# Attention and feed-forward layer: a zeroing matmul pair ahead of each y accumulation, and output stores moved six steps later in the down projection

## The reference, cut to what matters

```python
# attention without softmax: causal linear attention, 16 heads of 64
qkv = x @ Wqkv_w.T + Wqkv_b
scores = jnp.einsum('bhld,bhmd->bhlm', q, k * scale)
y = jnp.einsum('bhlm,bhmd->bhld', scores * causal, v)
a = y @ out_w.T + out_b
x = _layernorm(x + a)
# feed-forward, hidden 3072, int weights scaled by 1/127
h = jax.nn.silu(x @ wg.T) * (x @ wu.T)
x = _layernorm(x + h @ wd.T)
```

## Time and profile before

| what | us |
|---|---|
| median of 2 runs | 2166.96 (2164.74 to 2169.18) |
| the profiled execution, its own time | 2171.79 |
| span of its slowest core, the one shown (core 3) | 2170.2 |
| spans of the eight cores | 2148.2 to 2170.2 |
| mean granted TensorE clock, core 3 | 0.913 of full speed |

### The profile page before, as it was taken

One profiled execution on the slowest core, in us unless ns is written; L12 is line 12 of the kernel. 1 busy time (PEld: TensorE's weight loads), 2 busy tenths in 40 slices (PEclk: granted clock), 3 DMA queues, 4 the chain that ended last, 5 costly groups with the idle time before them and its releaser, 6 DMA issues.

```text
span 2170.2 us, 26434 instructions; the slowest of 8 cores (2148.2 to 2170.2 us)
## 1 busy us (share of the span) xinstructions
PE 1785.8 (82%) x9492; PEld 833.3 (38%) x9492; DVE 406.8 (19%) x803; ACT 400.3 (18%) x679; POOL 284.8 (13%) x263
## 2 busy tenths in 40 slices
PE   0775868998888788999868787999878778899985
PEld 0342433443334343444324343444333434344431
DVE  0212121121121222121121212212112122211111
ACT  0131221111013222111012223211101312211101
POOL 2032242100003121000002212000000302100001
PEclk9986989999888889999989897999989878899998
DMA  9119089974520102223541100322462010132264
GB/s 171 23 12 125 1 97 140 172 136 127 179 83 1 39 1 78 78 78 95 168 126 39 39 1 20 103 75 76 122 187 79 10 35 1 30 83 78 84 174 150
DMA packets 127935, 180.00 MB, mean 83 GB/s; under 512 B 58800, under 2 KB 58816, under 8 KB 127424
## 3 DMA queue, kind: packets, MB, share of 16 engines
q1 hardware_dynamic: 73728, 151.03, 24.0%
q0 software_dynamic: 54080, 27.28, 11.7%
HBM read 188.76 MB, written 35.65 MB: 103 GB/s over the span
## 4 chain that ended last, share of the span: by engine, by line
PE 69%; DMA 12%; DVE 6%; issue 5%; ACT 4%; POOL 3%; DVEq 0%; SPq 0%; ACTq 0%; POOLq 0%
PE pF L731 14%; PE pF L739 14%; PE pF L411 11%; PE pF L819 11%; PE pF L593 7%; PE pF L470 5%; DMA wdr<-wd_scr 5%; DMA wo_bf<-woT 2%; PE pF L386 2%; DMA wu_scr<-wuT 2%; ACT v_tm L478 2%; DVE h1f L639 1%; PE pF L513 1%; DMA wgr<-wg_scr 1%; ACT sqs L690 1%
## 5 line engine op out<-in xcount | busy, mean ns | idle before, releaser
L819 PE MATMUL pF<-wdr,h_fm 128*128 128x512 bf16 x1472 | 352.9, 397 | 59.4 <-DMA wdr<-wd_scr 58.7
L731 PE MATMUL pF<-x_fm,wgr 128*128 128x512 bf16 x1536 | 362.8, 379 | 10.2 <-DMA wgr<-wg_scr 6.4
L739 PE MATMUL pF<-x_fm,wur 128*128 128x512 bf16 x1536 | 362.8, 379 | 1.9 <-DMA wur<-wu_scr 1.9
L411 PE MATMUL pF<-x_fm,wqkv_bf 128*128 128x512 bf16 x1024 | 241.6, 401 | 13.2 <-DVE x_fm L396 8.1
L819 PEld LDWEIGHTS pF<-wdr,h_fm 128*128 128x128 bf16 x1472 | 143.9, 101 | 266.4 <-issue 121.1
L753 DVE TENSOR_TENSOR h_fm<-silu_s,pF 128x512 bf16<-128x512 bf16 x192 | 131.9, 687 | 531.9 <-PE pF L739 531.9
L731 PEld LDWEIGHTS pF<-x_fm,wgr 128*128 128x128 bf16 x1536 | 149.5, 98 | 191.3 <-issue 13.1
L739 PEld LDWEIGHTS pF<-x_fm,wur 128*128 128x128 bf16 x1536 | 150.0, 98 | 183.9 <-issue 3.9
L750 ACT ACTIVATE silu_s<-pF 128x512 bf16<-128x512 f32 x192 | 114.6, 597 | 549.9 <-PE pF L731 549.8
L593 PE MATMUL pF<-wo_bf,y_fm 128*128 128x512 bf16 x512 | 174.4, 516 | 0.0
L709 POOL TENSOR_SCALAR out_sb<-h1f,stats 128x1024 f32<-128x1024 f32 x32 | 38.2, 1193 | 993.3 <-DVE stats L707 980.9
(11 more groups left out here) (76 smaller groups left out, 943.4 us busy)
## 6 DMA issues: line engine op xcount, KB each, us to landing
wdr<-wd_scr SPq DMA_DIRECT2D x256, 256.0 KB, 3.2
wgr<-wg_scr SPq DMA_DIRECT2D x96, 256.0 KB, 2.7
wur<-wu_scr SPq DMA_DIRECT2D x96, 256.0 KB, 2.7
x_tm<-x SPq DMA_DIRECT2D x32, 512.0 KB, 4.6
out<-out_sb SPq DMA_DIRECT2D x32, 512.0 KB, 3.7
wqkv_bf<-wqkvT POOLq DMA_DIRECT2D x8, 768.0 KB, 24.9
wg_scr<-wgT POOLq DMA_DIRECT2D x24, 256.0 KB, 12.3
wu_scr<-wuT POOLq DMA_DIRECT2D x24, 256.0 KB, 12.6
```

The lines of the kernel that those rows point to most:

```text
L411: last = e.matmul(pF[:, b, :], wqkv_bf[:, kc, oc * P:(oc + 1) * P], x_fm[:, kc, :], start=(kc == 0), stop=(kc == DC - 1))
L731: last = e.matmul(pF[:, b, :], wgr[:, slot, kc, :], x1_fm[:, kc, t2 * 512:(t2 + 1) * 512], start=(kc == 0), stop=(kc == DC - 1))
L739: last = e.matmul(pF[:, b, :], wur[:, slot, kc, :], x1_fm[:, kc, t2 * 512:(t2 + 1) * 512], start=(kc == 0), stop=(kc == DC - 1))
L819: last = e.matmul(pF[:, 1 + 2 * j + n2, :], h_fm[:, hc, gc * P:(gc + 1) * P], wdr[:, slot, n2 * 512:(n2 + 1) * 512], start=False, stop=(id ...
```

## The change

Three edits. `y_zero_f` is now called in every chunk, with both banks as written, ahead of the state update; the matmuls of `y_intra_f` have no start flag any more; and a finalize is taken from `fin_q` only from step 6 of a group on (so at steps 6, 7 and 8).

```diff
@@ y_intra_f
                         v_tm[:, c, h * 64:(h + 1) * 64],
                         at_sb[:, at_slot(h), :],
-                        start=(pair % 4 == 0), stop=(g == 0),
+                        start=False, stop=(g == 0),
                         skip_group_check=True)
@@ a_tile_rest, chunk loop
             if c <= 3:
+                pl.op("pe", y_zero_f(), reads=[r_consts],
+                      writes=[rb[5], rb[6]])
                 if g < 15:
                     pl.op("pe", s_upd_f(c, g), reads=[r_k[c], r_v[c]],
                           writes=[rb[0]])
@@ sweep_b, down projection
                 wd_prefetch()
-                if fin_q:
+                if fin_q and idx >= 6:
                     fin_q.pop(0)()
```

## The result

| what | before | after |
|---|---|---|
| median, us | 2171.94 (32 runs) | 2186.5 (33 runs) |
| ratio after/before, 95% interval | | 1.0063 [1.0045, 1.008] |
| profiled execution, us | 2171.79 | 2170.46 |
| spans of the eight cores, us | 2148.2 to 2170.2 | 2139.1 to 2168.9 |

The change made the kernel 0.6% slower, 0.0063 x 2172 = 14 us. The forecast was 2165 with a range to 2186. "Within 2%" held; the sign did not. The medians are over all runs; the ratios leave out those in which the cores of a die ran some per cent longer at a lower clock.

What follows compares the result with a forecast made beforehand. TensorE, busy 1785.8 of 2170.2 us, was taken as the bound, through its idle time and clock. Stores -10 and zeroing pair +8 gave -2: 2169.8 for the profiled execution, 2165 against the median; range 2142 to 2186.

Steps and rivals of the forecast that it cites:

- Within 2%: Whole kernel: time stays within about 2%, 43 us, of before, between 2123.6 and 2210.3 us; chance 0.92.
- The stores: Down projection: later stores shorten stalls for weight blocks; 3.7 us per half, 15 in all as upper value, 10 taken.
- the 35 to 50 named: Down projection: L819's idle time behind weight loads should be 35 to 50 us after the change, not 58.7.
- the 3.9 us assumed: Down projection: a store was taken to land 3.9 us after its issue, as measured in a row before the change.
- The block only moves: Down projection rival: third store holds SP as long as before, nothing gained; 2167 + 8 = 2175 us, chance 0.25.
- The stores become free: Down projection rival: everything ready by step 6, landings overlap; 13 us per half, 53 in all, 2122 us, chance 0.05.
- The pair's chain: Attention chunks: zeroing pair and update behind L639 delay y; 0.2 to 0.3 us in 22 chunks, 8 us in all.
- The clock falls in the chunks: Attention chunks rival: idle time in one piece beside L639 tips L593 to half rate; up to 2215 us, chance 0.07.
- the clock rising: Attention chunks rival: the pair's added PE work brings every L593 to full rate; 62 us gone, 2103 us, chance 0.08.
- The sign chosen, L593: Attention chunks: L593's mean should stay between 490 and 540 ns; outside of that a clock rival holds.
- a quarter of the clock's price: Range: clock cases were taken to hold mostly in part, at a quarter of their price, -16 to +13 us.
- the 50 that I had priced: Attention chunks: price if L593 tips to half rate in all 32 chunks, 1.55 x 32 = 50 us.

Runs made afterwards that it cites:

- e1: Only the store edit (stores from step 6 of a group on) against the kernel before, chunks unchanged: ratio 0.9928, 16 us faster.
- e2: Only the one-row zeroing pair ahead of the state update, start flags removed, stores as before, against the kernel before: ratio 1.0118, 26 us slower.
- e5: Zeroing pair ahead of the state update made with 128 rows (identity times zeros), stores as before, against the kernel before: ratio 0.9892.
- e4: No zeroing pair and start flags as before; only the state update waits for L639 (banks 5 and 6), against the kernel before: ratio 0.9885.
- e16: Zeroing pair ahead of the state update made with 64 rows (half the identity times zeros), stores as before, against the kernel before: ratio 0.9897.
- e13: The kernel before with its one-row bias pair made with 128 rows (identity times the broadcast bias), no other edit: ratio 0.9861.
- e3: One-row zeroing pair placed behind the state update instead of ahead of it, stores as before, against the kernel before: ratio 0.9991.
- e9: State update waiting for L639, plus a one-row pair into banks 3 and 4 beside L639, against the kernel before: ratio 0.9936.
- e10: State update waiting for L639, plus a 128-row pair into banks 3 and 4 beside L639, against the kernel before: ratio 0.9946.

## Why the prediction was wrong

**The stores (-10, own account -15): right in mechanism, somewhat small.** The stall moved from steps 5 to 7 to steps 11 to 13, POOL waits 57.7 us for the store `out`, and PE's wait for blocks is 45.4, inside the 35 to 50 named. The gain by ratios is 16 us (e1) and 0.0118 - 0.0063 = 0.0055, 12 us (e2 to after); the two groups show 22 us in the one execution of after. Of that the stall is only (4.1 + 8.9 - 3.15 - 7.0) x 4 = 11.4. The rest goes with the clock, which rose from 0.946 to 0.974 over the second group and from 0.873 to 0.953 over the third (mean of cores and halves), and which my account left out. The landing of a store was longer than the 3.9 us assumed (5.5 in the second group shown, median 4.4 over all) and worked the other way. "The block only moves" is out by e1, whose gain is 16 [9, 22] us. "The stores become free" is out too: the third group still stalls for 7.0 us per half.

**The pair's chain (+8): the size was right where the clock held.** In chunks at full clock the distance is 9.30 us in e5 against 9.1 in e4: 0.2 us, as forecast. L579's idle time fell to 11.9 (I said about 8) and L524 waits 1.5 us in most of the 24 chunks (1.3 forecast, or 50 us with the two late ones; in this execution of after no chunk is late, so it is 35.9).

**The step that failed** is in the rival "The clock falls in the chunks", where the text says "Against: the new pair is work in the same place". With that the rival got 0.07, the forecast charged only the chain, and the clock stood in the sum at nothing. The runs show the opposite: with one row the pair makes the chunks slower than no pair at all, by 50 us (e2 against e4), and with 64 or 128 rows in the same time it does not (e16, e5). The pair alone cost 26 us, not 8. The rival's direction was right, and its reason and its place wrong. It blamed the idle stretch of L639 in one piece, and e4, which has just this stretch, is 25 us faster. It put the loss into L593, and the mean of L593 did not rise (515 ns before, 515 in e2); the matmuls ahead of it did. I also had the hint in the text, that the trace "does not say how a one-row matmul counts", and used it against the clock rising only. The earlier trace rows held another hint that I read as a duration: a one-row bias pair stands ahead of an L593 that ran at 516 ns mean, and in e13 128 rows there take it to 439.

**The sign chosen, L593, was the wrong one.** I wrote that a mean outside of 490 to 540 ns would show a clock rival. It came to 532 on the core shown and to 507 in the mean of the eight, inside both times, and the clock had fallen in half of the chunks all the same: the fall sits in L536, L552, L513 and L579. The distance from one L639 to the next shows it at once, 13.8 us against 9 to 12. I had named that one too, at 0.2 to 0.3 us longer, and it is the sign that came out wrong.

**The sum.** -16 for the stores and +26 for the pair make +10; measured is +14 [10, 17]. The range ended at 2186, on the reasoning that the clock holds in part, "a quarter of the clock's price". It took 26 - 8 = 18 us on top of the chain, a third of the 50 that I had priced. That the figure comes near is luck, since the 50 were worked out for L593. The miss of 21.5 us against 2165 has a second source: I started from 2167, the median of two runs, and 32 runs give 2172. So 5 us are the base, 18 the clock of the pair's chunks, -6 the stores, and 4 are left over.

## What to carry to other kernels

Where dense work follows, try a bias or a zero on all rows (identity times a broadcast tile) before the form with one row of contraction, or use the start flag. At two places of this kernel the one-row form cost 1.4% and more through the clock; behind the state update (e3) it cost nothing against before, and beside L639 128 rows were no better than one (e9, e10). So measure it at its place. Small work may go behind a wait as well as beside it: 16 update matmuls behind the wait gave 1.15%. And watch for stores that must wait in the queue that carries the loads: each way of moving them gave 0.7 to 1.1% here.

When two kernels are compared by their slowest cores, check a mean that moved little against all eight: L593 rose by 16 ns from core 3 to core 5 and fell by 8 over the cores.

## What the runs showed of the hardware that I had not expected

- Ahead of the state update, the granted clock of the chunks went with the rows of a matmul and not with its busy time: the pair at 1 row 1.0118, at 64 rows 0.9897, at 128 rows 0.9892, with the pair's own durations within 10% of each other. The bias pair ahead of L593 did the same (128 rows 0.9861). Beside L639 it did not (1 row 0.9936, 128 rows 0.9946).
- Chunks fall into a few lengths rather than a spread, each with its own mean clock: 9.1 to 9.7 us at 1.00, 10.5 to 11.1 at 0.84, 11.8 to 12.8 at about 0.72, and 13.4 to 14.2 at 0.63. In the 13.8-us chunk shown the clock stood at 0.50 in a stretch where PE was busy for 3.39 of 3.50 us, behind the 1.56 us of idle time and the one-row pair.
- The start of the update before or behind the wait changes a kernel by 1.15%, with the same instructions. Why a chunk takes one length or another with such a shift, and how many rows suffice between 1 and 64, the runs leave open.
